# Last phase of a four-part block on one core: quantised y turned by a transposing DMA as 16-bit floats instead of by fp32 transposes on PE, and its product one period later

## What is computed

```python
x = x + tanh(g_xattn[0]) * mha(layernorm(x), ctx, ctx, ...)          # phase 1 and the start of phase 2
x = x + tanh(g_ffn[0])   * bitlinear_ffn(layernorm(x), ...)          # phase 2
x = x + tanh(g_xattn[1]) * softmax(layernorm(x) @ ctx.T) @ ctx       # last phase
x = x + tanh(g_ffn[1])   * (mxfp4(layernorm(x)) @ mxfp4(weight).T + bias)   # last phase
```

## Time and profile before

| what | value |
|---|---|
| median of three runs | 1733.74 us (1730.14 to 1733.93) |
| the profiled execution's own time | 1735.12 us |
| its span in the trace | 1733.3 us |
| last phase in that span | from about 1411 us (its first DMA) to the end |
| PE, DVE, ACT, POOL busy over the whole span | 88%, 71%, 50%, 52% |
| fp32 transposes of y on PE (L1315 with `c_y`) | 128, mean 283 ns, 20.2 us busy |
| copies of turned y out of PSUM (ACT, L1413) | 32, mean 599 ns |

### The profile page before, as it was taken

One profiled execution on the slowest core, in us unless ns is written; L12 is line 12 of the kernel. 1 busy time (PEld: TensorE's weight loads), 2 busy tenths in 40 slices (PEclk: granted clock), 3 DMA queues, 4 the chain that ended last, 5 costly groups with the idle time before them and its releaser, 6 DMA issues. The chain is left out here.

```text
span 1733.3 us, 27279 instructions
## 1 busy us (share of the span) xinstructions
PE 1522.9 (88%) x7305; PEld 983.3 (57%) x7305; DVE 1230.2 (71%) x2149; ACT 873.9 (50%) x1433; POOL 905.4 (52%) x1162
## 2 busy tenths in 40 slices
PE   4789899998989999999726699999999938999997
PEld 3556565665656566565225355555555417888885
DVE  3566666776667677666476488888888826999985
ACT  3255455555555555545448455555555515555552
POOL 3166567656666765666600333434443215777774
PEclk9899999999999999998658899999999969999998
DMA  5826447382744638272090244444444344445420
GB/s 184 253 62 189 140 127 214 109 243 73 199 132 138 200 114 248 62 220 67 13 334 25 79 110 113 112 104 111 116 102 115 76 144 150 136 139 183 145 74 37
DMA packets 198401, 233.54 MB, mean 135 GB/s; under 512 B 97196, under 2 KB 114104, under 8 KB 194744
## 3 DMA queue, kind: packets, MB, share of 16 engines
q1 hardware_dynamic: 198328, 232.68, 46.3%
HBM read 135.86 MB, written 75.53 MB: 122 GB/s over the span
## 5 line engine op out<-in xcount | busy, mean ns | idle before, releaser
L501 ACT ACTIVATE a_probs<-a_sc 128x512 f32<-128x512 f32 x512 | 301.2, 596 | 312.3 <-PE a_sc L414 309.1
L556 DVE TENSOR_REDUCE a_negmax<-a_mx 128x1 f32<-128x512 f32 x512 | 336.7, 675 | 92.1 <-PE a_mx L397 90.4
L610 POOL TENSOR_TENSOR a_acc<-a_acc,a_probs 128x512 f32<-128x512 f32 x256 | 319.9, 1280 | 7.3 <-ACT a_probs L501 5.5
L610 POOL TENSOR_TENSOR a_acc<-a_probs 128x512 f32<-128x512 f32 x128 | 162.1, 1283 | 209.3 <-ACT a_probs L501 208.4
L397 PE MATMUL a_mx<-a_stack 96*128 96x512 f32 x512 | 229.0, 448 | 32.8 <-DVE a_negmax L556 19.9
L414 PE MATMUL a_sc<-a_stack 97*128 97x512 f32 x512 | 218.5, 429 | 18.1 <-DMA a_stack<-a_mrow 16.1
L993 PE MATMUL bank<-w_wgu,b_xq 128*128 128x512 bf16 x1024 | 228.1, 381 | 6.9 <-DMA b_xq<-b_xcode 6.7
L562 DVE RECIPROCAL a_attn<-a_den 128x128 f32<-128x128 f32 x128 | 120.8, 948 | 149.6 <-PE a_den L435 149.6
L993 PEld LDWEIGHTS bank<-w_wgu,b_xq 128*128 128x128 bf16 x1024 | 100.4, 98 | 129.7 <-DMA b_xq<-b_xcode 8.2
L397 PEld LDWEIGHTS a_mx<-a_stack 96*128 96x128 f32 x512 | 102.1, 199 | 104.9 <-DVE a_negmax L556 53.4
L1032 ACT ACTIVATE b_sig<-bank,b_tok 128x512 f32<-128x512 f32 x128 | 87.5, 683 | 91.6 <-PE bank L993 89.5
(11 more groups left out here) (177 smaller groups left out, 2657.1 us busy)
## 6 DMA issues: line engine op xcount, KB each, us to landing
a_stack<-spill SPq DMA_DIRECT2D x192, 256.0 KB, 4.9
spill<-a_part SPq DMA_DIRECT2D x64, 512.0 KB, 3.3
ctx_t<-a_ct SPq DMA_DIRECT2D x16, 1024.0 KB, 8.3
c_ct<-ctx_t SPq DMA_DIRECT2D x8, 2048.0 KB, 7.9
a_stage<-in_x_dram SPq DMA_DIRECT2D x32, 256.0 KB, 5.4
a_stage<-in_ctx_dram SPq DMA_DIRECT2D x32, 256.0 KB, 2.7
attn_t<-a_attn SPq DMA_DIRECT2D x32, 256.0 KB, 2.1
b_xin<-in_x_dram SPq DMA_DIRECT2D x32, 256.0 KB, 2.8
```

The lines of the kernel that those rows point to most:

```text
L501: nc.scalar.activation(probs[:, k, j, :], sc[i % 2][:], ACT.Exp, scale=SCALE).then_inc(exp_done, 1)
L556: nc.vector.tensor_reduce(negmax[:, g % 2, j, t:t + 1], mx[i % 2][:], axis=AX.X, op=ALU.max, negate=True).then_inc(mx_done, 1)
L610: nc.gpsimd.tensor_tensor(acc[:, j], probs[:, 0, j] if k == 1 else acc[:, j], probs[:, k, j], ALU.add)\
```

## The change

y after the quantisation is a 4-bit float times a power of two, which a bf16 number holds exactly. So:

- POOL's last multiplication (L1533) writes its result as bf16 into a new tile `ycode` instead of fp32 into `y`; ahead of it there is one more wait, for the transposing DMA two tiles back.
- A new step `yturn` on SP, at 336, issues one transposing DMA from `ycode` to `ycodet`; PE's four transposes of y go, and with them y's use of the turn banks.
- A new step `ycopy` on ACT, at 470, widens `ycodet` to fp32 in `yt`.
- The product `ffn` moves from 379 to 479, and `store` from 402 to 502: one period later, at the same place in the period.
- `Turns` has four banks for two users a tile. ACT's normalisation into `y` waits for `y_done` instead of `y_turned`, two tiles back.

```diff
@@ -1211,6 +1211,8 @@
         pt = sb("pt", [P, R2, T, 2, P], F32R)
         y = sb("y", [P, R2, D], F32)
         mag = sb("mag", [P, R2, D], BF16)
+        ycode = sb("ycode", [P, R2, D], BF16)
+        ycodet = sb("ycodet", [P, R2, C, P], BF16)
         yt = sb("yt", [P, R2, C, P], F32R)
         xo = sb("xo", [P, R2, D], F32)
 
@@ -1241,12 +1243,12 @@
         unit_ready, scaled_y, mag_done, quant_step = sem("unit_ready"), sem("scaled_y"), sem("mag_done"), sem("quant_step")
         ln_nmean, ln_bias = sem("ln_nmean"), sem("ln_bias")
         scale_step, scaled, rounded, y_done = (sem(n) for n in ("scale_step", "scaled", "rounded", "y_done"))
-        y_turned, yt_done, f_full, out_done = sem("y_turned"), sem("yt_done"), sem("f_full"), sem("out_done")
+        y_turned, yt_done, f_full, out_done = [sem(f"y_turned{i}") for i in range(R2)], sem("yt_done"), sem("f_full"), sem("out_done")
 
         W = 100
         at = dict(cload=-400, cload_step=99, csplit=-300, csplit_step=100, ctload=-420, xload=-190, norm=-70, xturn=-31,
                   score=0, recip=58, pturn=74, pv=132, ln2=175, norm2=206, scale=(216, 236, 238, 240), mag=288, quant=(300, 305, 310),
-                  yturn=364, ffn=379, store=402, max=34, exp=44, x3=35, out=23, act_turn=6, act_split=20, pool_split=30,
+                  yturn=336, ycopy=470, ffn=479, store=502, max=34, exp=44, x3=35, out=23, act_turn=6, act_split=20, pool_split=30,
                   dve_turn=13, pool_scale=4, pool_quant=8, pool_ln=0)
         ck = Clock(W * TT, NB // PAIR)
         for t in range(TT):
@@ -1258,7 +1260,7 @@
             if k == 0:
                 ck.add(first + at["ctload"], 9, "ctload", t)
             for rank, name in ((9, "xload"), (2, "xturn"), (3, "score"), (2, "pturn"), (4, "pv"), (8, "recip"),
-                               (2, "yturn"), (5, "ffn"), (9, "store")):
+                               (9, "yturn"), (2, "ycopy"), (5, "ffn"), (9, "store")):
                 ck.add(base + at[name], rank, name, t)
             for n in range(4):
                 ck.add(base + at["scale"][n], 7, "scale", t, n)
@@ -1271,11 +1273,11 @@
 
         def read_out(pe, it, shift, who):
             kind, t = who
-            for s in {"xturn": (x_hi, x_lo), "pturn": (p_hi, p_lo), "yturn": (yt_done,)}[kind]:
+            for s in {"xturn": (x_hi, x_lo), "pturn": (p_hi, p_lo)}[kind]:
                 wait_count(pe, s, it, shift, TT, t + 1)
 
-        turns = Turns(banks[0:3], [(shift, (name, *args)) for shift, name, args in ck.order()
-                                   if name in ("xturn", "pturn", "yturn")], NB // PAIR, read_out)
+        turns = Turns(banks[0:4], [(shift, (name, *args)) for shift, name, args in ck.order()
+                                   if name in ("xturn", "pturn")], NB // PAIR, read_out)
 
         with nc.Block() as block:
             @block.sync
@@ -1300,6 +1302,10 @@
                     elif name == "xload":
                         sync_wait(sp, held, out_done, it, shift, TT, t - XR + 1)
                         sp.dma_start(xr[:, t % XR, :], x[bass.ds(b, 1), rows, :]).then_inc(x_loaded[t % XR], 16)
+                    elif name == "yturn":
+                        sync_wait(sp, held, y_done, it, shift, TT, t + 1)
+                        sync_wait(sp, held, yt_done, it, shift, TT, t - 1)
+                        sp.dma_start_transpose(ycodet[:, t % R2], ycode[:, t % R2, :]).then_inc(y_turned[t % R2], 16)
                     elif name == "store":
                         sync_wait(sp, held, out_done, it, shift, TT, t + 1)
                         sp.dma_start(x_out[bass.ds(b, 1), rows, :], xo[:, t % R2, :]).then_inc(stored[t % R2], 16)
@@ -1324,9 +1330,6 @@
                     elif name == "pturn":
                         wait_count(pe, exp_done, it, shift, TT, t + 1)
                         turn(name, it, t, probs[:, t % R2, :], p_turned)
-                    elif name == "yturn":
-                        wait_count(pe, y_done, it, shift, TT, t + 1)
-                        turn(name, it, t, y[:, t % R2, :], y_turned)
                     elif name == "score":
                         wait_count(pe, x_lo, it, shift, TT, t + 1)
                         wait_count(pe, x_hi, it, shift, TT, t + 1)
@@ -1385,7 +1388,7 @@
                         wait_count(act, ln_bias, it, shift, TT, t + 1)
                         wait_count(act, ln_rstd, it, shift, TT, t + 1)
 
-                        wait_count(act, y_turned, it, shift, TT, t - 1)
+                        wait_count(act, y_done, it, shift, TT, t - 1)
                         nc.scalar.activation(y[:, t % R2, :], xr[:, t % XR, :], ACT.Identity, scale=rstd[:],
                                              bias=nbias[:]).then_inc(ln_done, 1)
                     elif name == "xturn":
@@ -1407,11 +1410,11 @@
                         wait_count(act, p_turned, it, shift, TT, t + 1)
                         wait_count(act, pv_full, it, shift, TT, t - 1)
                         nc.scalar.activation(pt[:, t % R2, :, HI, :], split(name, it, t), ACT.Copy).then_inc(p_hi, 1)
-                    elif name == "yturn":
-                        wait_count(act, y_turned, it, shift, TT, t + 1)
+                    elif name == "ycopy":
+                        wait_count(act, y_turned[t % R2], it, shift, TT // R2, t // R2 + 1, 16)
                         wait_count(act, f_full, it, shift, TT, t - 1)
-                        nc.scalar.activation(yt[:, t % R2], split(name, it, t), ACT.Copy).then_inc(yt_done, 1)
-                ck.run(act, window, dict(score=at["exp"], xturn=at["act_turn"], pturn=at["act_turn"], csplit=at["act_split"], yturn=at["act_turn"]))
+                        nc.scalar.activation(yt[:, t % R2], ycodet[:, t % R2], ACT.Copy).then_inc(yt_done, 1)
+                ck.run(act, window, dict(score=at["exp"], xturn=at["act_turn"], pturn=at["act_turn"], csplit=at["act_split"]))
 
             @block.vector
             def _(dve):
@@ -1530,7 +1533,8 @@
                     elif name == "quant" and args[1] == 2:
                         wait_count(pool, rounded, it, shift, TT, t + 1)
                         wait_count(pool, scale_step, it, shift, TT * 3, 3 * t + 3)
-                        nc.gpsimd.tensor_tensor(blocks(y[:, t % R2, :]), blocks(y[:, t % R2, :]), spread(blk[:, t % R2, 1]),
+                        wait_count(pool, y_turned[t % R2], it, shift, TT // R2, t // R2, 16)
+                        nc.gpsimd.tensor_tensor(blocks(ycode[:, t % R2, :]), blocks(y[:, t % R2, :]), spread(blk[:, t % R2, 1]),
                                                 ALU.mult).then_inc(y_done, 1)
                 ck.run(pool, window, dict(scale=at["pool_scale"], quant=at["pool_quant"], ln=at["pool_ln"], csplit=at["pool_split"]))
```

## The result

| | before | after |
|---|---|---|
| median of 11 runs each, us | 1733.74 (1730.14 to 1739.05) | 1724.16 (1718.43 to 1733.67, and one of 1869.96) |
| ratio, 95% interval | | 0.9947 (0.9931 to 0.9963) |
| profiled execution and its span, us | 1735.1, 1733.3 | 1723.4, 1721.6 |
| first score product to the end of the span, us | 304.8 | 294.2 |

The changed kernel is 9.6 us faster by the medians and 11.7 by the spans of the two profiled executions. Forecast were 11.0, and 1722.7 us for the median; the last phase alone, the last row, is 10.6 us shorter. One execution of the changed kernel took 1869.96 us at a mean granted clock of 0.784 instead of about 0.94; the ratio leaves it out, and without it the median is 1723.85.

A forecast was written before the change was run, and what follows sets the result against it. PE was taken to set the period of 27 tiles, with DVE and a shared cycle close behind; 10.5 (period) + 0.5 (first period) + 0.0 (end) = 11.0 us off 1733.7 gave 1722.7 us, range 1719.3 to 1729.5.

The forecast's parts named there:

- PE sets the period, and loses 0.44 us: Last phase, each tile: PE's period falls from 8.73 to 8.29 us as four of twelve transposes go.
- Rival D: Last phase: PE's transposes weren't in the way, so the period stays 8.74; no chance of its own.
- Three cycles meet, I take 8.35: Loop period: PE 8.29, DVE 8.29, shared cycle 8.32 meet; 8.35 taken between 8.30 and 8.42, saving 10.5 us.
- the shared one: Cycle through PE and DVE: score product, value product, addition, statistics, low part of next turned x; 8.32 us.
- DVE's own cycle is 8.29: Last phase: 8.74 less DVE's 0.45 us wait before its addition, so at most 0.45 could come off PE.
- First period 0.5: Tile 3 to tile 4: falls from 8.84 to 8.32 us as the last product begins later, 0.5 us less.
- The end 0.0: After the last score product: 1.3 us gained at DVE's addition between roundings, 1.3 lost on the DMA path.
- The low end of the range: Fastest time expected: period 8.30, 12.4 us gained, 1721.3, less 2 us for run spread: 1719.3.
- rival B: POOL's L1533 in the loop: a 16-bit write over 1.5 us makes it slower, 1749 at 2.1 us; chance 0.07.
- rival C: Transposing DMA: slower than in the phase before, by SP's queue or longer landing, 1725.1 or 1726.7 us; chance 0.08.
- rival A: Loop: DVE's rounding L1464 meets POOL's small work; 1728.1 us at half price, 1733 with all; chance 0.19.

The follow-up runs named there:

- the shift alone: The kernel before with only the last product and the store one period later, no DMA transpose: 1734.5 us, ratio to before 0.9992.

## Why the prediction was right, point by point

**PE sets the period, and loses 0.44 us.** The transposes take just that less. But the 8.74 was not all PE's: 0.08 of it was the last product waiting for ACT inside its own group, which the shift removes. The forecast's PE bound of 8.29 should have been 8.22. Only the shift alone showed it: 1.87 for the same eight matmuls. Rival D, that the transposes weren't in the way, falls with the run in which four were put back and 0.30 us a tile with them.

**Three cycles meet, I take 8.35.** Measured 8.361 and 8.377. The reasoning "8.29, 8.29 and 8.32 meet, so a little above" gave the right number with the wrong mix: the 0.03 us added to the longest of the three was a guess, and that it nearly fits is in part luck. It is one cycle, the shared one, that sets 8.36, with PE 0.14 us under it. Tile 3 had shown it alone at 8.32; in the middle of the loop it is 8.34 to 8.37, but for two periods of 8.46 and 8.55, and the last seven periods, where no context tile is split any more, are back at 8.31 to 8.34. Which of the context steps costs these 0.04 us stays open; it is not POOL's subtraction, without which the period was the same.

**DVE's own cycle is 8.29.** As a number it was met, by luck: the ring through DVE stops every faster variant at 8.29. As a reason it does not hold. In the kernel before, from which it was read, DVE's cycle already held 0.81 us in which L1452 and L1454 were held by POOL (708 + 484 ns against 207 + 175 without the conflict); after, it is 0.58 (660 + 299), and a wait for y has come in. Busy time is not work where two engines can hold each other.

**First period 0.5.** 0.52.

**The end 0.0.** It is a loss of 0.2, and both halves came about as argued, 1.6 us gained and 1.45 lost where 1.3 and 1.3 were forecast. The timeline of the end, beside the earlier trace rows:

```profile
1707.24 1.10 DVE L1467 SCALAR_TENSOR_TENSOR c_y<-c_mag,c_y 128x512 f32<-128x512 bf16 x1 [2.12 <-ACT c_mag L1402]
...
1708.26 0.74 DVE L1494 SCALAR_TENSOR_TENSOR c_xo<-bank,w_cact,c_xr 128x512 f32<-128x512 f32 x1
...
1710.13 1.05 POOL L1537 TENSOR_TENSOR c_ycode<-c_y,c_blk 128x512 bf16<-128x512 f32 x1 [2.35 <-DVE c_y L1473]
...
1713.80 0.63 ACT L1416 ACTIVATE c_yt<-c_ycodet 128x512 fp32r<-128x512 bf16 x1 [6.07 <-DMA c_ycodet<-c_ycode]
...
1714.48 3.68 PE L1361 MATMUL bank<-w_w,c_yt 128*128 128x512 f32 x8 [3.24 <-ACT c_yt L1416]
```

DVE's addition no longer waits between the roundings (1.28 us before); from the last score product to the end of POOL's last multiplication it is 25.5 us instead of 27.1. From the end of L1537, 1711.18, to the last product it is 3.30 us where 3.15 were forecast. The last score product to this one is 28.8 us, forecast about 29. What was missed is that the last product itself takes 3.68 instead of 3.44 us. Both ran at the lower clock, before for most of its length, after for nearly all of it.

**The low end of the range** is added up as 12.1 + 0.5 = 12.4 us; 27 x 0.44 is 11.9, so 12.4, and the 1721.3 that follows from it, stand.

**POOL's 16-bit write (rival B)** is 1051 ns against 1050: no price at all. (The trace before did hold one POOL instruction that writes 16 bits, a MEMSET of 128x1; no full-width one.) **The DMA path (rival C)** lands in 2.4 us in the median (5.6 at most), four blocks of 128x128, and delays ACT once. The 5.2 us estimated from the Trainium skill, page "VectorE: DVE Perf Modes" (The three transpose paths), did not come; the phase before had already shown the right number for the same shape.

**DVE and POOL in each other's way (rival A)** happened, with the roles turned round, and was there before the change too, where nmean was the one held (510 ns, now 238). The forecast watched DVE's rounding, which stayed at 709 ns (708 before). The one held was POOL:

```profile
1569.33 0.68 DVE L1467 SCALAR_TENSOR_TENSOR c_y<-c_mag,c_y 128x512 f32<-128x512 bf16 x1
```

```profile
1569.49 0.93 POOL L1514 TENSOR_TENSOR c_rstd<-c_veps,w_mhalf 128x1 f32<-128x1 f32 x1
```

L1467 started first and kept its 0.68; L1514, 0.55 before, ended at 1570.42. It delays y, and DVE's wait for y lies in the slack that the shared cycle leaves DVE. The Trainium skill, page "SBUF — State Buffer" (Who interferes with whom), says that whoever issues first holds the shared ports and the other blocks; these rows agree, and so does L1455, held by POOL until POOL's end. The price is less than the whole length here: L1514 ends 0.41 us behind L1467, with 0.55 of its own. The forecast had drawn from its rule only the case in which DVE comes second.

## What to carry to other kernels

Before counting a piece of the critical chain as work, compare it with the same instructions where their operand is surely early: a wait of less than 0.1 us hides inside a matmul group. If an engine is relieved, write down every closed cycle through it and its neighbours with its length; the next longest is the new period, and the cheapest further gain is the step in that cycle that nobody in it needs (here `bn_aggr`, 3 us for one moved line). A transposing DMA in place of transposes on a full PE paid here only with its consumer a period later: the same DMA without the shift made this kernel 0.9% slower.

## What the hardware showed that I had not expected

A two-operand DVE instruction holds POOL's instructions on one number per row for several tenths of a us, and which of them is held changes with the timing: before the change it was nmean (510 ns), after it rstd and nbias (549 to 836 ns, 259 to 506, nmean down to 238). If the order on POOL is changed, the next one in line is held (`veps` 215 to 528 ns). DVE's `tensor_scalar` on 16 fp32 numbers per row is held by POOL in turn, 207 to 660 ns.

PE's clock for the last product differs between kernels that end in the same instructions. Mean granted clock is the first number behind POOL's busy time; after, and in the kernel with the four transposes put back:

```profile
1715.00:1717.00 2.00, 2.00 (x6) 1.54 (x5) 0.00 (x0) 0.00 (x0) 0.00 (x0) 0.50 0.00 0
```

```profile
1722.00:1724.30 2.30, 2.13 (x8) 1.42 (x8) 0.03 (x1) 0.05 (x1) 0.00 (x0) 1.00 0.29 114
```

Behind a product at 1.00 and 3.24 us without a matmul, the clock of the changed kernel fell as the last product began; it ran at 0.50, 1.2 GHz, and took 3.68 us. In the other kernel the product ahead of it had run at 0.50 itself and ended only 1.57 us earlier; the clock rose at that product's end, and the last one ran at 1.00, 2.4 GHz, and took 2.13. The shift alone shows the same as the latter: 0.94 us behind a product of 3.76, the last one took 2.11. A short gap alone does not give the high clock: in the kernel before, the last product began 0.69 us behind four transposes, at 0.50, and took 3.44. Between 3.68 and 2.13 lie 1.55 us at the very end, more than either term that the forecast weighed there.
